# The last slot of a transformer kernel: one batch's gated result taken in two halves, filler products in TensorE's gap, and the last two outputs combined from PSUM

## The reference, cut to what matters

```python
    x = x + _L1_attn_ref(_layernorm(x), ...)      # retention, 4 heads, then a gated group norm and the product with Wo
    x = x + 0.5 * _L1_ffn_ref(_layernorm(x), ...) # mixture of depths

# in _L1_attn_ref: o is (B, T, 4, 64)
        o = o * lax.rsqrt(mean(o * o, -1) + EPS) * gnorm_w
        o = o * (g * jax.nn.sigmoid(g))
        return o.reshape(B, T, 256) @ Wo.T

# in _L1_ffn_ref: k = 256 of the 512 tokens of each batch
        scores = einsum('bsd,d->bs', hidden, w_router)
        top_scores, top_idx = lax.top_k(scores, k)
        h = gelu(selected @ W1 + b1);  processed = h @ W2 + b2
        output = hidden + scatter(sigmoid(top_scores) * processed)
```

## Time and profile before

| | |
|---|---|
| median of 3 runs | 805.19 us (804.76 to 806.33) |
| the profiled execution | 807.99 us, of which the span from first to last instruction is 805.8 us |
| PE busy in the span | 757.8 us, 94% |
| DVE busy | 665.8 us, 83% |
| ACT busy | 424.5 us, 53% |
| POOL busy | 475.3 us, 59% |
| mean granted TensorE clock | 0.977 of full |

### The profile page before, as it was taken

The page is one execution under the profiler, slowest core; times in us unless marked ns, Lnnn a source line. Parts: engine busy times, 40 slices in busy tenths (PEclk is TensorE's granted clock), DMA queues, the critical chain, the costliest instruction groups (busy, mean ns, idle before and its releaser), DMA issues.

```text
span 805.8 us, 29577 instructions
## 1 busy us (share of the span) xinstructions
PE 757.8 (94%) x13001; PEld 614.8 (76%) x13001; DVE 665.8 (83%) x1825; ACT 424.5 (53%) x875; POOL 475.3 (59%) x375
## 2 busy tenths in 40 slices
PE   5778999999999999998999999999999999999875
PEld 4666888787887787776878888877888888878653
DVE  6686888888888999997858889987777988888887
ACT  2333555565555565654554446655544565564745
POOL 4467888887888888876543444444434344453544
PEclk9996999999999999999999999999999999999988
DMA  7000100011111110010000000000000000000113
GB/s 229 30 28 29 29 28 16 16 28 29 29 28 30 28 29 2 3 55 3 1 2 2 3 3 2 2 2 2 3 2 2 3 2 2 3 2 16 55 39 105
DMA packets 23284, 18.57 MB, mean 23 GB/s; under 512 B 2146, under 2 KB 20468, under 8 KB 22900
## 3 DMA queue, kind: packets, MB, share of 16 engines
q1 hardware_dynamic: 22596, 16.40, 7.0%
q10 hardware_dynamic: 560, 0.28, 0.1%
HBM read 12.48 MB, written 4.19 MB: 21 GB/s over the span
## 4 chain that ended last, share of the span: by engine, by line
PE 75%; DVE 17%; POOL 3%; ACT 2%; issue 1%; DMA 0%; DVEq 0%; POOLq 0%; ACTq 0%
PE ps L286 20%; PE ps L410 11%; PE ps L401 10%; PE ps L281 5%; PE ps L675 4%; PE ps L364 3%; PE ps L308 3%; PE ps L297 3%; PE ps L384 3%; PE ps L394 2%; POOL grstd L1067 2%; PE ps L356 2%; DVE x L1225 2%; PE ps L667 2%; PE ps L320 2%; PE ps L685 2%
## 5 line engine op out<-in xcount | busy, mean ns | idle before, releaser
L1067 POOL TENSOR_TENSOR grstd<-gve,mhalf 128x32 f32<-128x32 f32 (+1 forms) x32 | 159.0, 4968 | 26.5 <-DVE gve L1280 26.5
L410 PEld LDWEIGHTS ps<-w_s,hid 128*128 128x128 f32 x1024 | 123.5, 192 | 9.0 <-issue 8.0
L410 PE MATMUL ps<-w_s,hid 128*128 128x128 f32 x1024 | 129.0, 277 | 0.7 <-issue 0.7
L401 PE MATMUL ps<-xt_r,w_s 128*128 128x512 f32 x256 | 126.7, 617 | 0.7 <-ACT xt_r L822 0.7
L826 ACT ACTIVATE hid<-ps,b_s 128x512 f32<-128x512 f32 x128 | 84.0, 726 | 24.0 <-PE ps L401 23.8
L1063 POOL TENSOR_TENSOR r_ret<-ve_ret,powers 128x8 f32<-128x8 f32 x32 | 57.8, 1807 | 27.6 <-DVE ve_ret L1211 27.6
L286 PE MATMUL ps<-w_qkvg,xt_p 128*128 128x128 f32 x512 | 71.2, 285 | 2.8 <-ACT xt_p L822 2.8
L1073 POOL TENSOR_TENSOR um<-um 128x96 f32<-128x96 f32 (+1 forms) x32 | 21.3, 665 | 88.5 <-DVE um L1259 88.5
L401 PEld LDWEIGHTS ps<-xt_r,w_s 128*128 128x128 f32 x256 | 45.2, 192 | 35.1 <-issue 30.1
L1058 POOL TENSOR_TENSOR rstd_ln_mod<-ve_ln_mod,mhalf 128x4 f32<-128x4 f32 x32 | 32.3, 1010 | 65.3 <-DVE ve_ln_mod L1211 65.3
L1253 DVE TENSOR_TENSOR sc<-ps,tri 128x1024 f32<-128x1024 f32 (+1 forms) x64 | 58.3, 953 | 15.1 <-PE ps L320 7.6
(11 more groups left out here) (236 smaller groups left out, 1749.8 us busy)
## 6 DMA issues: line engine op xcount, KB each, us to landing
xtin<-in_xt SPq DMA_DIRECT2D x16, 256.0 KB, 3.8
out_x<-base SPq DMA_DIRECT2D x16, 256.0 KB, 2.3
xin<-in_x SPq DMA_DIRECT2D x15, 256.0 KB, 3.0
rot<-in_rot SPq DMA_DIRECT2D x2, 1024.0 KB, 5.9
w_s<-in_w SPq DMA_DIRECT2D x2, 256.0 KB
xin<-in_x ACTq DMA_DIRECT2D x1, 256.0 KB, 4.0
w_qkvg<-in_wqkvg SPq DMA_DIRECT2D x1, 256.0 KB, 3.8
w_qkv<-in_wqkv SPq DMA_DIRECT2D x1, 256.0 KB
```

The source lines that it names most:

```text
L401: nc.tensor.matmul(bank(k), w1_s[:, f, :], xt["r"][:].rearrange("p j n -> p (j n)"), start=True, stop=True).then_inc(s[f"h{f}"], 1)
L410: mm = nc.tensor.matmul(bank(k, j * P, P), hid[:, f, j * P:(j + 1) * P], w2_s[:, f, :], start=False, stop=(f == last and j == NT - 1), ski ...
L1067: nc.gpsimd.tensor_tensor(grstd[:, 0:n], gve[:, 0:n], mhalf[:, 0:n], ALU.pow) \
```

## The change: what it does

All of it but two small items is in `slot_end`.

1. **Batch 15 in halves of two token tiles.** `transpose_y` signals after each half, ACT squares each half, DVE sums each (`half_sums`), POOL takes two roots of 8 columns in place of one of 16. DVE multiplies y by the gate while POOL works (`yg`) and then each half by its root (`normed_half`). PE transposes and multiplies by Wo half by half (`gated_half`, `output_half`); ACT copies in halves.
2. **Order.** PE's attention waits behind half of batch 14's output product. Batch 15's output product comes before `routed_up(1)`. On DVE x2 of batch 15 and its variance move ahead of the narrowing of round 3; `base_weights(1)`, which begins with `negative_mean` of batch 15 and so waits for `ln_mod_rstd`, stands between `rank_try(4)` and `rank_narrow(3, 4)`. PE's and POOL's orders named above stay as they were: `rank_sum(3, 5)` is still ahead of `last_rows(14)` and the products down, and the third `add_output` is still ahead of batch 15's root.
3. **Filler.** `keep_busy(18, X1)` issues 18 products of the identity with itself, read by nobody, after `transpose_y`; `keep_busy(5, 2)` issues five in the very first slot.
4. **Base on ACT.** The base of batches 14 and 15 is an ACT activation of x2 with a scale and a bias (`scaled_base`), for which DVE prepares two small tiles; DVE's `keep_base` for them is gone.
5. **Masks by products.** Group 3's two masks are no longer added on DVE and transposed: `group_mask` multiplies each by a narrow selector (`sel_f` float32, `sel_l` bfloat16) and sums in PSUM. DVE forms the mask steps in four instructions in place of five, and two instructions at the start (`prepare_rest`) make the selectors.
6. **Results from PSUM.** `store_y` for batches 14 and 15 is gone. DVE combines batch 15 from bank 2; ACT scales batch 14 in place in bank 5, and DVE adds it from there.

```diff
 PE slot_end
+                output_b(old, (2,))
                 for c in range(NT):
                     attend_b(c, c == NT - 1, sl)
-                output_b(old, (2, 3))
+                output_b(old, (3,))
                 rank_sum(3, 1, 1)
-                transpose_y(now)
+                ... (the same transposes, y_half after each half)
+                keep_busy(18, X1)
                 wait(pe, "ln_mod_xn", old)
                 transpose4("ln_mod", h, X2)
-                rank_sum(3, 2, 1)
+                gated_half(0)
                 wait(pe, "ln_mod_xt", old)
                 routed_up(0, X1)
+                rank_sum(3, 2, 1)
+                gated_half(1)
+                output_half(0)
+                output_half(1)
+                rank_sum(3, 3, 1)
                 routed_up(1, 3)
-                transpose_gated(now, YB)
-                rank_sum(3, 3, 1)
                 wait(pe, "act0", old)
                 routed_up(2, X1)
-                output_b(now, (0, 1))
                 rank_sum(3, 4, 1)
-                output_b(now, (2, 3))
                 wait(pe, "act1", old)
                 routed_up(3, 3)
                 rank_sum(3, 5, 1)
                 last_rows(LAST, YB)
...
                 last_rows(NB - 1, YB)
-                rank_mask(3, YB + 1)
+                wait(pe, "k_over", 1)
+                group_mask(msk_a, sel_f[:], 2, True)
+                wait(pe, "k_mask", 4)
+                group_mask(picked, sel_l[:], 2, False).then_inc(s["k_mt"], 1)
                 last_column(NB - 1, 0)
+    def keep_busy(times, k):
+        for _ in range(times):
+            nc.tensor.matmul(bank(k, 0, P), ident, ident, start=True, stop=True)
 PE slot_a
+                if g < 0:
+                    keep_busy(5, 2)
 ACT slot_end
                 route_weight(3)
+                copy_half(0)
                 hidden(0, X1, old)
+                copy_half(1)
+                scaled_base(sl.batch(-1), x2, 0, old)
                 hidden(1, 3, old)
-                copy_gated(now, YB)
                 hidden(2, X1, old)
                 weigh(7)
                 hidden(3, 3, old)
-                normalise(now)
+                normalise(now, x2b)
                 copy_xt("ln_mod", xt["r"], X2, now)
-                store_y(2, sl.batch(-1), old)
+                scaled_base(sl.batch(0), x2b, 1, now)
 POOL slot_end
                 root("ln_mod", old)
-                group_root(4 * H1, now)
-                wait(pool, "gy", now)
+                (two powers of 8 columns, each after gve_half)
+                wait(pool, "gy_half", 2)
                 for n in range(3, 6):
                     add_output(n)
                 root("ln_mod", now)
 DVE slot_end
+    def base_weights(n, count):
+        negative_mean(count)
+        nc.vector.tensor_scalar(base_w[:, n, 0, :], rstd["ln_mod"][:], 0.5, 1.0, ALU.mult, ALU.add)
+        wait(dve, "nmr", count)
+        nc.vector.tensor_scalar(base_w[:, n, 1, :], nmr[:], 0.5, None, ALU.mult).then_inc(s["base_w"], 1)
-                head_sums(H1, V1, sl)
-                negative_mean(old)
+                half_sums(0, sl)
+                half_sums(1, sl)
+                base_weights(0, old)
+                (t2 = y * gate, in two halves, each signals yg)
+                normed_half(0)
                 rank_narrow(3, 1, 1)
                 rank_try(2)
-                keep_base(sl.batch(-1), old)
-                head_norm(H1, V1, now)
-                (t2 = t2 * gate)
+                normed_half(1)
                 rank_narrow(3, 2, 1)
                 rank_try(3)
+                scaled_sum(..., x2b, "wo", "x2", now)
+                variance("ln_mod", x2b, ve["ln_mod"], now)
                 rank_narrow(3, 3, 1)
                 rank_try(4)
+                base_weights(1, now)
                 rank_narrow(3, 4, 1)
                 rank_try(5)
-                wait(dve, "base", old)
-                scaled_sum(..., x2, "wo", "x2", now)
-                variance("ln_mod", x2, ve["ln_mod"], now)
                 rank_narrow(3, 5, 1)
-                rank_above()
-                negative_mean(now)
-                rank_between()
-                rank_order()
-                rank_choose()
-                keep_base(sl.batch(0), now)
+                (msk_a -> k_over; msk_b; scan that starts at cnt; picked -> k_mask)
...
-                output(NB - 1)
+                wait(dve, "mod", 2 * NB)
+                (four combines of batch 15, one operand from bank 2)
                 wait(dve, "weighted", 1)
-                nc.vector.tensor_tensor(base[:, at], base[:, at], yall[:, at], ALU.add)
+                nc.vector.tensor_tensor(base[:, at], bank(YB + 1), base[:, at], ALU.add)
```

More of the change, by code:

```diff
@@ L110, in program @@
         sel_b = sb("sel_b", [P, 2], BF16)
+        sel_f = sb("sel_f", [P, GB])
+        sel_l = sb("sel_l", [P, GB], BF16)
         wr_f = sb("wr_f", [P, FEW])
@@ L479, in last_mask, with group_mask @@
                 return mm
+            def group_mask(src, to, k, first):
+                for j in range(NT):
+                    mm = nc.tensor.matmul(bank(k, GB * j, GB), src[:, j * P:(j + 1) * P], to,
+                                          start=(first and j == 0), stop=not first, skip_group_check=True)
+                return mm
             def rank_bank(g, behind=1):
@@ L743, in slot_b, with gated_half, output_half @@
                 states_b((0, 1), True, BT["state"], sl)
+            def gated_half(half):
+                wait(pe, "gy_half", half + 1)
+                for j in range(2):
+                    for k in range(2):
+                        at = (2 * half + j) * VF + k * P
+                        mm = nc.tensor.transpose(bank(YB + half, (2 * j + k) * P, P), t2[:, at:at + P], ident)
+                mm.then_inc(s["tg_half"], 1)
+            def output_half(half):
+                wait(pe, "gt_half", half + 1)
+                for j in (2 * half, 2 * half + 1):
+                    for k in range(2):
+                        mm = nc.tensor.matmul(bank(BT["wo"], j * P, P), gt[:, k, j * P:(j + 1) * P], w_o1[:, k, :],
+                                              start=(k == 0), stop=(k == 1), skip_group_check=True)
+                if half == 1:
+                    mm.then_inc(s["wo"], 1)
             def slot_end(sl):
@@ L758, in slot_end @@
                 rank_sum(3, 0, 1)
+                output_b(old, (2,))
                 for c in range(NT):
                     attend_b(c, c == NT - 1, sl)
-                output_b(old, (2, 3))
+                output_b(old, (3,))
                 rank_sum(3, 1, 1)
-                transpose_y(now)
+                wait(pe, "ycopy", now)
+                for half in range(2):
+                    for c in (2 * half, 2 * half + 1):
+                        for k in range(2):
+                            at = YB * BANK + c * VF + k * P
+                            mm = nc.tensor.transpose(PS[:, at:at + P], qm[:, k, c * P:(c + 1) * P], ident)
+                    mm.then_inc(s["y_half"], 1)
+                keep_busy(18, X1)
                 wait(pe, "ln_mod_xn", old)
@@ L804, in slot_end @@
                 last_sum(2, 1)
-                wait(pe, "ystore", old)
+                wait(pe, "k_bank", 4 * (ROUNDS + 2))
                 routed_down(0, 2, now)
@@ L1011, in slot_b, with copy_half, scaled_base @@
                 queries_b(BT["tqk"], sl)
+            def copy_half(half):
+                wait(act, "tg_half", half + 1)
+                nc.scalar.copy(gt[:, :, 2 * half * P:2 * (half + 1) * P].rearrange("p k (j n) -> p j k n", j=2),
+                               bank(YB + half).rearrange("p (j k n) -> p j k n", j=2, k=2)).then_inc(s["gt_half"], 1)
+            def scaled_base(b, src, n, count):
+                wait(act, "base_w", n + 1)
+                for j in range(NT):
+                    last = nc.scalar.activation(base[:, b * S + j * P:b * S + (j + 1) * P], src[:, j, :], ACT.Identity,
+                                                bias=base_w[:, n, 1, j:j + 1], scale=base_w[:, n, 0, j:j + 1])
+                last.then_inc(s["base"], 1)
             def slot_end(sl):
@@ L1021, in slot_end @@
                 weigh(5)
-                wait(act, "ytok", now)
-                nc.scalar.activation(sq[:], PS[:, YB * BANK:(YB + 2) * BANK], ACT.Square).then_inc(s["sq"], 1)
+                for half in range(2):
+                    wait(act, "y_half", half + 1)
+                    nc.scalar.activation(sq[:, half * S:(half + 1) * S], bank(YB + half), ACT.Square) \
+                        .then_inc(s["sq_half"], 1)
                 weigh(6)
@@ L1047, in slot_end @@
                 weigh(GB + 4)
-                store_y(2, sl.batch(0), now)
             run_slots(slot_a, slot_ab, slot_b, slot_end)
             act.wait_ge(s["k_weight"], 1)
-            weigh(LAST, "weighted")
+            wait(act, "mod", 2 * NB - 1)
+            for j in range(NT):
```

(12 more changed lines are left out.)

76 lines of the change are left out of this document (60 added, 16 removed).

## The result

Ten executions of each kernel gave a median of **810.3 us** for the changed kernel (807.17 to 814.1) and 804.98 for the one before (801.84 to 809.13): ratio 1.0058, interval 1.0034 to 1.0082. (A ratio here is estimated from all executions of both kernels and is not the quotient of the two medians, which is 1.0066.) The change makes the kernel 0.6% slower. The forecast was 810.4.

The account below looks back on a forecast made before the run. The last slot was taken as a relay with no engine full, its end following K. Terms +2.4, +2.4, +0.7, 0 and -0.3 sum to +5.2 us, on the median of 805.19 giving 810.4 us; range 806.3 to 812.5.

Parts of the forecast that it names:

- slot: Last slot, from the first carry product to the span's end; the forecast's terms there come to +5.5 us.
- queue behind `rank_sum(3, 5)`: On PE: `rank_sum(3, 5)` moves from 778.11 to 781.5, and 7.5 us of work with it; +2.4 us.
- half clock in the gap: PE's thin work from 775.4 to 781.5 drops its clock to half, about 779.7 to 786.4; +2.4 us.
- K: End of PE's second `last_rows`, when the search for batches 14 and 15 can start; 786.48 before, forecast 791.3.
- K to `weigh(8)`: From K to ACT's `weigh(8)`: narrow mask products +0.6, one `last_sum` earlier in PE's queue +0.1; +0.7 us.
- combine from PSUM: Batch 15's four combines cost DVE 1.0 us less, but POOL's end opens the stores; 0.
- first slot: Five fillers in PE's idle 1.9 us may prevent the clock's fall at 22.0; 0 to -0.65, taken as -0.3 us.
- The relay: Last slot, engine to engine: x2 of batch 15 4.4 us earlier, 2.2 lost in POOL's queue, try 5 3.5 later.
- The rival without a held root: `weigh(7)` comes by 775, POOL's root ends at 777.4: 805.9 us, no change; chance 0.09.
- PE's two gaps: PE idle above 2 us each before `rank_sum(3, 4)` and `rank_sum(3, 5)`, the second at about 781.5.
- The fillers: 18 products on PE from 763.7 to 768.1, 4.4 us, delay nothing and hold the clock at full.
- The rival in which they don't hold it: PE's stretch 766.0 to 772.6 stays at half clock, `wo` comes a little later: 811.3 us; chance 0.07.

Follow-up runs that it names:

- weights_later: Changed kernel with DVE's `base_weights(1)` moved behind `rank_try(5)`; 805.92 us, ratio 1.0008 to the kernel before.
- fill_gap: Changed kernel with 8 and 10 more filler products in PE's gaps ahead of `rank_sum(3, 4)` and `rank_sum(3, 5)`; 808.62 us, ratio 1.0032 to the kernel before.
- changed_again: Changed kernel, unaltered, timed and profiled once more; 810.97 us, ratio 1.0051 to the kernel before.
- before_fill18: Kernel before the change with only the 18 filler products added after `transpose_y`; 804.85 us, ratio 0.9992 to the kernel before.
- root_first: Changed kernel with POOL's root of batch 15 ahead of the third `add_output`; 808.91 us, ratio 1.0038 to the kernel before.
- no_fill5: Changed kernel without the five filler products of the first slot; 811.23 us, ratio 1.0064 to the kernel before.
- old_masks: Changed kernel with group 3's masks added on DVE and transposed by PE as before the change; 809.75 us, ratio 1.0037 to the kernel before.
- fill_transposes: Changed kernel with the 18 filler products replaced by 36 transposes of the identity; 811.08 us, ratio 1.0056 to the kernel before.
- down_first: Changed kernel with PE's `last_rows(14)`, products down 0 to 2 and `last_column(14)` ahead of `rank_sum(3, 5)`; 806.72 us, ratio 1.0012 to the kernel before.

## Why the prediction was right, point by point

The sum of the prediction was +5.2 us; the medians differ by 5.3, and the ratio gives 4.7 (2.7 to 6.6 by its interval). The terms, against the slot of the profiled execution:

| term | forecast | measured |
|---|---|---|
| queue behind `rank_sum(3, 5)` | +2.4 | +2.7 |
| half clock in the gap | +2.4 | +1.5 (2.3 to 2.9 in four other profiles) |
| K to `weigh(8)` | +0.7 | +0.7 |
| combine from PSUM | 0 | -0.1 |
| slot | +5.5 | +4.85 |
| first slot | -0.3 | not resolved |

The first two come from K: +4.18 in the slot. From `rank_sum(3, 5)` to K were 8.86 us, and 7.40 and 7.41 where the clock stayed full (weights_later, fill_gap); the difference, 1.46, is the clock, and 4.18 less 1.46 is the queue.

That the total came within 0.1 us is luck; the order of the waits and their causes are not. The queue was forecast 0.3 too low and the clock 0.9 too high. The interval is 4 us wide, the changed kernel's second profile had a slot longer by 7.3 us and not 4.85, and over the twelve edited kernels, changed_again among them, the slots lie further above 47.61 than the ratios account for, by 1.3 us in the mean. before_fill18, in which the first part of the program is untouched, shows the same 1.3, so this is no sign of a gain elsewhere; the one profile of the kernel before may just have a short slot.

- **The relay.** As forecast in its order and its causes: POOL idle before the third `add_output`, the root behind it, DVE idle 1.95 us (forecast 2), `rank_sum(3, 5)` 3.7 later (3.4). x2 was 3.9 earlier, not 4.4 (3.6 to 4.6 over the profiles in which the fillers stood and the order up to there was the changed kernel's), and the root 1.8 earlier, not 2.2. That the third `add_output`, and so `weigh(7)`, held the root is shown by root_first, where it went to wait for the variance instead; that the wait on DVE matters is shown by weights_later. The rival without a held root was worked out as 0.7 us above the median before; weights_later, which takes away what the held root does to DVE, came out 0.08% above the one before, 0.6 us.
- **PE's two gaps.** 2.42 and 1.50 us; forecast above 2 each. The second is shorter because `routed_up(3)` ran at half clock, 2.06 us. changed_again and no_fill5 had 2.42 and 2.46.
- **The clock.** It fell 20.0 us in the slot and lasted 6.8 us (forecast 21.5 and 6.6). The loss is 1.5 and not 2.4 since the fall came 1.5 earlier, so more of it lay in the idle part. changed_again, no_fill5, old_masks and fill_transposes, alike in this place, lost 2.4, 2.5, 2.3 and 2.9, so the term is a range of 1.5 to 2.9 from one execution to the next. The forecast's reason, that every fall follows a thin stretch, stood on one fall of its rows (766.0). The trace bears it out for the other two, more weakly: PE was busy for 1.74 us of 18.6 to 22.0 and of 59.5 to 62.9. fill_gap goes against it (below). Not foreseen was a second fall, behind K, in changed_again (787.8 to 791.2): `weigh(8)` came 6.05 us after K there, 1.5 more than in the first profile.
- **The fillers.** The filled stretch has full clock, as forecast, and 36 records took 4.18 us (4.4). The rival in which they don't hold it is out, and so is the doubt whether only real products would: transposes do as well.
- **K to `weigh(8)`.** Sum and split are right: 0.60 for the narrow products by the start of `routed_up(0)`, and 0.1 for `last_sum(0)`. What the forecast does not say is that the first hides a wait of the second, so that only 0.27 comes back when the masks alone are undone.
- **The combine from PSUM.** 1.12 us for four, from 2.15 (forecast 1.13), and POOL's last instruction ends at 800.53, after DVE's 800.18: nothing at the end, as forecast. That POOL's end opened the last three stores before the change was not quite so: SP waited 0.3 and 0.2 us there for DVE's two results as well, and for neither in the changed kernel. From `weigh(8)` to POOL's end are 10.89 (10.98).
- **The two roots of 8 columns.** 3.24 us for two, 1.62 each; forecast 1.65 to 1.81.
- **The selector steps.** Taken as hidden. The second one took 1.25 us, not 0.17, and the products of the rotation behind it started later (below): at 32.63, 31.28 before, with PE's work of the second slot behind them. By DVE's next sum it is some 0.4 us (34.91 against 34.52), in a part where nothing smaller than the shifts of the clock can be seen in the median, so it stays open whether they reach the end.

## What to carry to other kernels

In a relay of engines with queues in order, the lead that one step gains is worth only what stands first in the next queue lets through: look for the instruction that waits, and at what is queued behind it, on every engine that the lead passes. Here three small DVE instructions moved behind one search round were worth 4 us of slot (1.5 of them a fall of the clock that did not come), and products moved ahead of the waiting search sums, with POOL's order changed to match, turned a loss of 0.6% into a gain of 0.4%. Fill a gap of TensorE with work of the kernel itself before filling it with products that nobody reads: in the gap before K the filler kept the clock and left the ratio at 1.0032, the kernel's own work brought it to 1.0012, though these intervals overlap.

## What the runs showed of the hardware

- **The lock between DVE and POOL.** In the first slot of the changed kernel, DVE's and then POOL's timeline:

```profile
31.14 0.17 DVE L1558 TENSOR_SCALAR sel_f<-yall 128x8 f32<-128x8 f32 x1
31.35 1.25 DVE L1559 TENSOR_SCALAR sel_l<-yall 128x8 bf16<-128x8 f32 x1
32.63 1.22 DVE L1303 TENSOR_TENSOR ra<-ps,rot 128x1024 f32<-128x1024 f32 x1
```

```profile
31.30 1.26 POOL L1162 TENSOR_TENSOR xb<-xin,bias_b 128x512 f32<-128x512 f32 x1
```

  A step of 8 columns lasted as long as POOL's instruction that had started 0.05 us ahead of it, though its twin took 0.17. `negative_mean` of root_first, 4 columns, did the same (1.02 against 0.16). The Trainium skill (SBUF — State Buffer, SBUF: two separate sides) says that a DVE instruction with two SBUF inputs and a GpSimd one that reads SBUF exclude each other for a whole instruction. `negative_mean` agrees with it: 1.02 us, ended with POOL's. `sel_l` has one tensor input, and it waited too. The same section names a second case, a DVE instruction in a perf mode that uses both ports; `sel_l` may be one, but no run here shows its mode.
- **A fall without a gap.** In fill_gap the clock fell at 788.4 behind 3.9 us in which PE's records leave no idle time (3.90 busy of 3.90), with 20 of the 32 records products of 8 or 1 columns. (The ends of PE's records are modelled, so short idle times could be missing.) It fell in that place in changed_again and down_first too, in down_first behind 0.96 us of idle time, and not in the first profile of the changed kernel. Whether the narrow products are the reason was not tried.
